# Attention stage: turned rows and logits in two places, a new order of work on TensorE and ScalarE

## The reference

```python
x = x + s * g                               # first layer; s needs out = H @ Wo.T + bo
xn = _layernorm(x, axis=-1)
q = (x @ Wq.T + bq).reshape(S, B, HEADS, D_K)          # x is xn here; k and v alike
scores = jnp.einsum('ibhd,jbhd->ijbh', q, k) / np.sqrt(D_K)
scores = jnp.where(causal, scores, -jnp.inf)
attn = softmax_one(scores, axis=1)          # exp / (1 + sum of exp)
out = jnp.einsum('ijbh,jbhd->ibhd', attn, v)
...
logits = xt @ wg                            # of the same xn, for the router
```

## Time and profile before

| | |
|---|---|
| median of 3 runs | 1421.14 us (1421.1 to 1423.01) |
| the profiled execution | 1429.75 us, of which 1427.9 us from the first to the last instruction |
| TensorE's mean granted clock | 0.935 of full |
| the attention stage in the trace | about 269.8 us (first output product) to 574.7 us (POOL's last sum) |

### The profile page before, as it was taken

How to read it: one execution, slowest core, us unless ns; L and a number is a source line. 1 busy time by engine, 2 the same in 40 slices (tenths; PEclk the granted TensorE clock), 3 DMA queues, 4 the chain that set the end, 5 groups by cost and what they waited for, 6 DMA issues and landing times. The chain is left out here.

```text
span 1427.9 us, 22572 instructions
## 1 busy us (share of the span) xinstructions
PE 1175.3 (82%) x7547; PEld 802.9 (56%) x7547; DVE 1016.6 (71%) x1931; ACT 628.1 (44%) x960; POOL 625.2 (44%) x530
## 2 busy tenths in 40 slices
PE   4899999588888884146999989999899998999910
PEld 3566666366666663134566666666666665666610
DVE  7757667759888887885767667676576765776638
ACT  4855555233333441003544545445455454553522
POOL 5500000028777777013454544645546455464430
PEclk9999999799999997557999999999999999999965
DMA  8260000001111110105555445554555545555569
GB/s 328 83 214 1 1 1 1 15 30 31 31 31 31 32 31 16 59 19 109 105 109 104 76 99 101 112 106 71 108 92 113 109 66 114 89 111 104 66 168 347
DMA packets 148960, 122.55 MB, mean 86 GB/s; under 512 B 88400, under 2 KB 133328, under 8 KB 148720
## 3 DMA queue, kind: packets, MB, share of 16 engines
q1 hardware_dynamic: 114912, 83.90, 20.1%
q0 software_dynamic: 25200, 35.85, 16.4%
q10 hardware_dynamic: 8736, 1.33, 0.5%
HBM read 58.91 MB, written 44.30 MB: 72 GB/s over the span
## 5 line engine op out<-in xcount | busy, mean ns | idle before, releaser
L1722 ACT ACTIVATE e_h_all<-e_pH,e_b1c,e_h_scale 128x512 f32<-128x512 f32 x256 | 199.6, 780 | 283.9 <-PE e_pH L1763 256.1
L1777 PE MATMUL e_pY<-e_w_hi,e_h_hi 128*128 128x256 f16 x1024 | 279.6, 273 | 17.1 <-DVE e_w_lo L1597 10.0
L1506 POOL DMA_INDIRECT e_xg<-xn_rows,e_icol x140 | 162.4, 1160 | 287.1 <-DVE e_icol L1538 254.3
L1778 PE MATMUL e_pY<-e_w_lo,e_h_hi 128*128 128x256 f16 x1024 | 279.1, 273 | 0.0
L1779 PE MATMUL e_pY<-e_w_hi,e_h_lo 128*128 128x256 f16 x1024 | 279.1, 273 | 0.0
L1521 POOL DMA_INDIRECT expert_sums<-e_yo,e_dcol x128 | 213.0, 1664 | 76.7 <-issue 43.0
L1640 DVE TENSOR_TENSOR e_h_lo<-e_h_all,e_h_hi 128x512 f16<-128x512 f32 x256 | 177.3, 693 | 66.3 <-ACT e_h_hi L1722 56.6
L1761 PE MATMUL e_pH<-e_xT,e_w_hi 128*128 128x512 f16 x512 | 195.1, 381 | 26.5 <-DMA e_xT<-e_xs 17.6
L1762 PE MATMUL e_pH<-e_xT,e_w_hi 128*128 128x512 f16 x512 | 194.9, 381 | 0.0
L1763 PE MATMUL e_pH<-e_xT,e_w_lo 128*128 128x512 f16 x512 | 194.8, 380 | 0.0
L1777 PEld LDWEIGHTS e_pY<-e_w_hi,e_h_hi 128*128 128x128 f16 x1024 | 100.1, 98 | 42.9 <-DVE e_h_lo L1640 24.6
(11 more groups left out here) (251 smaller groups left out, 2169.0 us busy)
## 6 DMA issues: line engine op xcount, KB each, us to landing
raw<-expert_w SPq DMA_DIRECT2D x18, 1024.0 KB
expert_sums<-a_zero SPq DMA_DIRECT2D x10, 1024.0 KB, 10.7
x_st<-x SPq DMA_DIRECT2D x16, 512.0 KB, 9.1
xn_rows<-c_xn SPq DMA_DIRECT2D x16, 512.0 KB, 3.0
f_ya<-expert_sums SPq DMA_DIRECT2D x16, 512.0 KB, 7.3
out<-x_st SPq DMA_DIRECT2D x8, 1024.0 KB, 8.5
e_xg<-xn_rows,e_icol POOLq DMA_INDIRECT x140
e_xT<-e_xs SPq DMA_TRANSPOSE x136
```

The costliest lines, as they stand in the source:

```text
L1506: pool.indirect_dma_start(xg[:, q, 0:D + E], None, v.xn3_dram, bass.IndirectOffsetOnAxis(icol[u][:, q:q + 1], axis=0), bounds_check=N - 1, ...
L1722: last = act.activation(dst, pH[h % NPH][:, :], ACT.Relu, bias=b1c[eu][:, h:h + 1], scale=h_scale[eu][:, 0:1])
L1777: pe.matmul(pY[:, q, :], h_hi[:, h, cols], w2_hi[:, h, :], start=(h == 0), stop=False)
L1778: pe.matmul(pY[:, q, :], h_hi[:, h, cols], w2_lo[:, h, :], start=False, stop=False)
```

## The change

The turned rows xnT, the logits' PSUM place pL and the copy lgT get two places each, used in turn by even and odd tiles; k, which had two copies, gets one. PE's order within a tile becomes: queries, keys, turn of the next tile, values, logits, output of the tile after next, and the turn of the logits of the tile before. ACT's order follows it. The core of the diff:

```diff
-        xnT = sb("c_xnT", [P, KD, BANK])
+        xnT = [sb(f"c_xnT{n}", [P, KD, BANK]) for n in range(2)]
-        k = [sb(f"c_k{n}", [P, B, D]) for n in range(2)]
+        k = sb("c_k", [P, B, D])
-        lgT = sb("c_lgT", [P, P])
+        lgT = [sb(f"c_lgT{n}", [P, P]) for n in range(2)]
-        pL = psum("c_pL", [P, BANK])
+        pL = [psum(f"c_pL{n}", [P, BANK]) for n in range(2)]
...
                 def body(i, u, left):
                     t = 2 * i + u
-                    put_logits(t)
                     act.wait_ge(ex_in, t + 1)
                     act.activation(ex[:, :, :, :], ex[:, :, :, :], ACT.Exp).then_inc(ex_out, 1)
-                    store_logits(t)
+                    take_logits(t)
+                    if t:
+                        put_logits(t - 1)
+                        store_logits(t - 1)
                     if left >= 2:
                         normalise(t + 2, u, i + 1)
+                        take_turned(t + 2)
                     if left >= 1:
-                        take_logits(t + 1)
                         take_v(t + 1, 1 - u)
                     if left >= 2:
-                        take(xnT, pT, t_done, t_evac, t + 2)
                         take_qk(t + 2, u)
+                    if left == 0:
+                        put_logits(t)
+                        store_logits(t)
...
                 def body(i, u, left):
                     t = 2 * i + u
                     pe.wait_ge(t_evac, t + 1)
...
+                    pe.wait_ge(v_evac, t + 1)
+                    product(0, pY, q_done, t)
+                    pe.wait_ge(op_ready, t + 2 if left >= 1 else t + 1)
+                    product(1, pX, k_done, t)
                     if left >= 1:
                         turn(t + 1, 1 - u)
-                    pe.wait_ge(l_taken, t + 1)
-                    pe.transpose(pL[:, P:2 * P], lgT[:, :], ident).then_inc(l_turned, 1)
+                    pe.wait_ge(q_evac, t + 1)
+                    product(2, pY, v_done, t)
+                    logits(t)
+                    if left >= 2:
+                        pe.wait_ge(k_evac, t + 1)
+                        output(t + 2)
+                    if t:
+                        turn_logits(t - 1)
+                    if left == 0:
+                        turn_logits(t)
```

More of the change, by code:

```diff
@@ L1003, in body @@
                         last = dve.tensor_tensor(qk[:, PAIR0[j]:PAIR0[j] + w, :], q[:, j:B, :],
-                                                 spread(k[u][:, j, :], w), ALU.mult)
+                                                 spread(k[:, j, :], w), ALU.mult)
                     last.then_inc(sm, 1)
@@ L1052, in take_logits @@
                     act.sem_inc(passed, 1)
-                    act.activation(lgT[:, :], pL[:, 0:P], ACT.Copy).then_inc(l_taken, 1)
+                    if t >= 2:
+                        act.wait_ge(l_turned, t - 1)
+                    act.activation(lgT[t % 2][:, :], pL[t % 2][:, 0:P], ACT.Copy).then_inc(l_taken, 1)
                 def put_logits(t):
@@ L1058, in put_logits @@
                     act.activation(v.logit_st[:, :, t, :],
-                                   pL[:, P:2 * P].rearrange("p (b e) -> p b e", e=GRP)[:, :, 0:E],
+                                   pL[t % 2][:, P:2 * P].rearrange("p (b e) -> p b e", e=GRP)[:, :, 0:E],
                                    ACT.Copy).then_inc(l_evac, 1)
@@ L1075, in take_qk @@
                     take(q, pY, q_done, q_evac, t, scale=DK ** -0.5)
-                    take(k[u], pX, k_done, k_evac, t)
+                    take(k, pX, k_done, k_evac, t)
                 def take_v(t, u, reused=True):
@@ L1081, in take_v, with take_turned @@
                     take(vv[u], pY, v_done, v_evac, t)
+                def take_turned(t):
+                    take(xnT[t % 2], pT, t_done, t_evac, t)
                 normalise(0, 0, 0)
-                take(xnT, pT, t_done, t_evac, 0)
+                take_turned(0)
                 normalise(1, 1, 0)
                 take_qk(0, 0, reused=False)
-                take_logits(0)
+                take_turned(1)
                 take_v(0, 0, reused=False)
-                take(xnT, pT, t_done, t_evac, 1)
                 take_qk(1, 1)
@@ L1125, in turn, with logits, turn_logits, product @@
                     last.then_inc(t_done, 1)
+                def logits(t):
+                    if t >= 2:
+                        pe.wait_ge(l_evac, t - 1)
+                    for kk in range(KD):
+                        for b in range(B):
+                            last = pe.matmul(pL[t % 2][GRP * b:GRP * b + GRP, 0:P], v.wgr[:, kk, :],
+                                             xnT[t % 2][:, kk, b * P:(b + 1) * P], start=(kk == 0), stop=(kk == KD - 1))
+                    last.then_inc(l_done, 1)
+                def turn_logits(t):
+                    pe.wait_ge(l_taken, t + 1)
+                    pe.transpose(pL[t % 2][:, P:2 * P], lgT[t % 2][:, :], ident).then_inc(l_turned, 1)
+                def product(n, dst, done, t):
+                    for m in range(2):
+                        pe.matmul(dst[:, 2 * m:2 * m + 2, :], ones3[:, :], spread(bias3[:, n * D:(n + 1) * D], 2),
+                                  start=True, stop=False, skip_group_check=True)
+                    for b in range(B):
+                        for kk in range(KD):
+                            last = pe.matmul(dst[:, b, :], xnT[t % 2][:, kk, b * P:(b + 1) * P],
+                                             v.wqkv[:, kk, n * D:(n + 1) * D], start=False, stop=(kk == KD - 1),
+                                             skip_group_check=True)
+                    last.then_inc(done, 1)
                 output(0)
@@ L1135, in body @@
                     pe.wait_ge(t_evac, t + 1)
[L1136 to L1163, removed]
```

## The result

The changed kernel takes 1516.66 us (median of 4, 1515.21 to 1518.52) against 1421.37 us before: 1.0669 times as long, interval 1.065 to 1.0687. The forecast was 1531 us, range 1509 to 1553.

What follows compares the result with a forecast made beforehand. PE, DVE and POOL were nearly full at 16.98 us a tile; the new order's chain takes 22.2 plus 2.8 for the clock, 25.0. Over 13 periods +104, with head and tail +110: 1531 us, range 1509 to 1553.

Steps and rivals of the forecast that it cites:

- The ring: Chain output, layer0, exp, normalise, turn, v, logits, next output across PE, DVE and ACT: must now fit one tile's time, not two.
- Its sum at full clock: Chain's links from layer0 to layer0 one tile on: 22.2 us a tile at full clock, against 16.98 before.
- the DVE chain: Layer0 and attention on DVE to the end of the subtraction: 11.97 us taken, rather than 13.76 beside POOL's products.
- The clock's term: Turn and v on PE begin at the lower clock after some 7 us idle: 2.8 us lost per tile, period 25.0.
- the two rows: Earlier clock rises, 8.3 us after the turn started and 4.3 after a first matmul: losses between 2.2 and 4.15 us a tile.
- the forecast's own range: Total time by the clock's loss per tile: 2.2 us gives 1523, 4.15 us gives 1549; chance 0.81.
- its margin for a sooner rise: Stated range extended down to 1509 us, as a clock rise sooner than any row shows was not excluded.
- Head and tail: Stage's start and end: output(2) behind turn(1) and v(0), +4.4 us; from layer0(15) to tile 14's weights some 35 us, +2.5.
- The clock stays full: Rival: PE's clock never falls, 22.2 us a tile, +74 us, so 1495 us; chance 0.06.
- POOL's products stay: Rival: POOL's products still fall on DVE's q times k, 26.8 us a tile, 1554 us; chance 0.08.
- The change does what its buffers allow: Rival: PE loses its 2.5 us of waits, DVE sets the pace at 15.8 us a tile, -19, 1402 us; chance 0.03.
- both waits of the earlier trace: PE's waits per tile for the logits' copy (1.2 us) and turned rows' copy (1.1 to 1.4), about 2.5 us to win.

## Why the prediction was right

- **The ring.** Right in every link: released by the rows it named, in its order, and cut where the runs cut it. Putting the turn back gave 106.6 us of the stage; the double places and single keys, without the turn's place, cost nothing.
- **Its sum at full clock**, 22.2 us: the run with PE kept busy had 21.97. The choice of the DVE chain beside a POOL with only small work was right: 11.71 us for 11.97, q times k 3.00 us, POOL waiting in scale for the statistics; scale's small instruction beside it (1.09 us from 401.78) did not lengthen it. The Trainium skill, "SBUF — State Buffer", section "Who interferes with whom", has the rule that the two share a port pair under an exclusive lock. The trace agrees: in the run with the output early, where a sum of POOL's products (419.48 to 421.28) reaches into it, q times k took 4.12 us again.
- **The clock's term is what was mis-sized**: 2.8 us a tile were taken, "between the two rows", and 1.92 to 1.94 measured, below the lower row's 2.2. So 1516.66 lies under the forecast's own range of 1523 to 1549, and layer0's distance of 23.89 just under the 24 to 26 named as a sign; the result is inside the stated range only by its margin for a sooner rise. The clock's term makes 0.9 of the 1.1 us by which the period of 25.0 was too long; 0.34 is the DVE chain and the way to the normalising, which were a little shorter, and the mean over the tiles is 0.1 above the tile read. 13 x 1.1 = 14 us is the whole miss: 96.1 us of the stage for 110. The Trainium skill, "TensorE: Matmul & The Clock Gate", section "HAM oscillation — how this bites in real kernels", puts the loss at half of the time that work runs throttled. The trace agrees: half of 4.05 is 2.0, and 1.94 was measured.
- **Head and tail**: +4.4 forecast, 301.46 - 270.09 against 296.77 - 269.76 is +4.36; +2.5 forecast, +1.8 measured (59.07 us from layer0(15) to POOL's end for 57.24); the terms of that sum give 34.4, rounded to 35, so unrounded +1.9.
- **The rivals.** *The clock stays full* gave 1495, and the run that kept it full came to 1498.74. *POOL's products stay* is out by q times k. *The change does what its buffers allow* is out for this order, but with the turn put back it is what happened, at half its size: 10 us for 19. The prediction counted both waits of the earlier trace rows as waits for a place; in the order of before, the one for the turned rows is a wait for the data.

A ring was cut twice, and each time a longer list showed another behind it: without the output behind the turn 19.79 us a tile (ACT's copy of k ahead of the exp), without the exp ahead of the normalising 19.85 (the same copy ahead of the normalising). Of the edits tried on the changed kernel, only putting the turn back takes the period below 16.98.

## What to carry to other kernels

A second buffer permits an order; it doesn't make it good. Before a step is moved up on an in-order engine, follow its input back through every engine's list until the chain meets a result of the moved engine, and count over how many tiles the ring runs: here the same chain went from two tiles' time to one. And ask of each wait that a buffer should remove whether it is for the place or for the data: the first gave 10 us when the place was doubled alone, the second nothing.

## What had not been expected of the hardware

The prediction had not reckoned with this: the rise of the clock does not keep a fixed distance to the work that follows the idleness. In the tiles read it came 4.05 us after the turn's start in the changed kernel, 5.92 when the turn came 0.95 us earlier in the ring. The period hardly moved (23.89 and 23.78; in the last seven periods 23.89 in both), so an edit that shortens such a ring can measure as nothing while the clock falls in each tile, and as all of its 0.93 us when it doesn't. What sets the moment of the rise, these runs don't show.
